# Perceiver layer on one core: GpSimd zero-writes between the 32 scatters of token rows to the experts

## The reference, cut to what matters

```python
logits = flat @ router_w.T
topk_scores, topk_idx = jax.lax.top_k(logits + router_bias, TOPK)      # TOPK = 2
topk_scores = jax.nn.softmax(topk_scores, axis=-1)
...
up_all = jnp.einsum('nd,kde->nke', flat, up_proj)
gate_all = jnp.einsum('nd,kde->nke', flat, gate_proj)
hidden = jax.nn.silu(gate_all) * up_all
down_all = jnp.einsum('nke,ked->nkd', hidden, down_proj)
out = jnp.einsum('nk,nkd->nd', combine, down_all)
sh_hidden = jax.nn.silu(flat @ sh_gate.T) * (flat @ sh_up.T)
out = out + sh_hidden @ sh_down.T
```

## Time and profile before

| what | value |
|---|---|
| three runs | 553.18, 553.84 and 561.45 us, median 553.84 us |
| profiled execution, its own time | 555.59 us |
| its span, from first to last instruction | 553.9 us |
| share of the span: PE, PEld, DVE, ACT, POOL | 89%, 61%, 71%, 34%, 36% |
| scatters, from the first start to the last end | 395.75 to 436.98 us |
| first tile loaded, first matmul of the experts | 438.63 and 440.83 us |

### The profile page before, as it was taken

The page is one execution under the profiler, slowest core; times in us unless marked ns, Lnnn a source line. Parts: engine busy times, 40 slices in busy tenths (PEclk is TensorE's granted clock), DMA queues, the critical chain, the costliest instruction groups (busy, mean ns, idle before and its releaser), DMA issues.

```text
span 553.9 us, 14401 instructions
## 1 busy us (share of the span) xinstructions
PE 493.0 (89%) x4952; PEld 335.8 (61%) x4953; DVE 394.4 (71%) x1038; ACT 190.6 (34%) x589; POOL 199.0 (36%) x302
## 2 busy tenths in 40 slices
PE   7897999999999999999997999999999299999900
PEld 7664666656656666666654666665466178888700
DVE  3798799999899999999544888887653135555525
ACT  3244332343323332333313455553200045555400
POOL 4000314011222222222115677773377435555520
PEclk9999999999999999999999999999999689999955
DMA  7999679877978888873128996700023334444258
GB/s 279 353 340 263 205 229 310 274 220 216 303 240 286 287 287 288 294 256 107 40 70 241 261 266 190 222 1 2 33 100 106 106 112 137 126 140 139 61 185 269
DMA packets 67296, 108.65 MB, mean 196 GB/s; under 512 B 8195, under 2 KB 49077, under 8 KB 67256
## 3 DMA queue, kind: packets, MB, share of 16 engines
q1 hardware_dynamic: 60840, 97.70, 56.7%
q0 software_dynamic: 3792, 8.43, 4.4%
q10 hardware_dynamic: 2624, 1.97, 1.1%
HBM read 85.31 MB, written 24.72 MB: 199 GB/s over the span
## 4 chain that ended last, share of the span: by engine, by line
PE 65%; DMA 10%; DVE 7%; POOL 7%; issue 6%; ACT 3%; SPq 1%; ACTq 0%; POOLq 0%; DVEq 0%
PE banks L1065 15%; PE banks L1041 14%; PE banks L1424 8%; DMA ring<-in_ctx_dram 7%; POOL rows_by_expert L711 6%; PE banks L1436 4%; DVE ctxT L1529 3%; PE banks L1053 3%; PE banks L1418 2%; PE banks L1000 2%; PE banks L1078 2%; DMA xn_all<-expert_out 2%; PE banks L1174 2%; PE banks L1181 2%; PE banks L1086 2%
## 5 line engine op out<-in xcount | busy, mean ns | idle before, releaser
L1529 DVE STREAM_TRANSPOSE ctxT<-ring 128x832 f32<-128x832 f32 x128 | 121.8, 1009 | 5.5 <-DMA ring<-in_ctx_dram 5.5
L1041 PE MATMUL banks<-ctxT,qT_all 32*64 32x416 f32 (+2 forms) x2048 | 93.9, 498 | 2.0 <-issue 1.2
L1065 PE MATMUL banks<-ring,prob 128*64 128x256 f32 (+1 forms) x832 | 93.6, 381 | 0.7 <-ACT prob L795 0.7
L1065 PEld LDWEIGHTS banks<-ring,prob 128*64 128x64 f32 (+1 forms) x832 | 58.6, 137 | 31.5 <-issue 4.2
L1041 PEld LDWEIGHTS banks<-ctxT,qT_all 32*64 32x64 f32 x2048 | 56.8, 131 | 30.7 <-issue 13.6
L611 POOL TENSOR_TENSOR var<-mv,eps 128x1 f32<-128x1 f32 x32 | 6.3, 196 | 168.9 <-DVE mv L1574 116.8
L717 POOL DMA_INDIRECT expert_out<-prob,dest x47 | 46.2, 984 | 46.4 <-DVE prob L1892 28.2
L808 ACT ACTIVATE prob<-banks,negmax 128x416 f32<-128x416 f32 (+2 forms) x80 | 41.0, 530 | 30.2 <-DVE negmax L1551 30.2
L1424 PE MATMUL banks<-ring,ctxT 128*128 x188 | 50.5, 392 | 0.3 <-ACT ctxT L919 0.3
L1885 DVE TENSOR_TENSOR ctxT<-banks,ctxT 128x128 f32<-128x128 f32 x47 | 13.7, 292 | 42.0 <-ACT ctxT L922 41.2
L795 ACT COPY prob<-banks 128x512 f32<-128x512 f32 x64 | 27.6, 515 | 38.9 <-PE banks L1053 38.9
(11 more groups left out here) (245 smaller groups left out, 876.6 us busy)
## 6 DMA issues: line engine op xcount, KB each, us to landing
ring<-in_ctx_dram SPq DMA_DIRECT2D x48, 1024.0 KB
qT_all<-q_by_pair SPq DMA_DIRECT2D x56, 128.0 KB, 8.9
ctxT<-rows_by_expert SPq DMA_DIRECT2D x47, 129.0 KB, 2.1
rows_by_expert<-blank SPq DMA_DIRECT2D x12, 387.0 KB, 4.4
mid<-stage SPq DMA_DIRECT2D x31, 128.0 KB, 2.3
ring<-in_ctx_dram SPq DMA_DIRECT2D x16, 130.0 KB
ctxT<-mid SPq DMA_DIRECT2D x16, 128.0 KB, 2.8
qT_all<-mid SPq DMA_DIRECT2D x16, 128.0 KB, 3.1
```

Of the source, the lines that this page charges most:

```text
L1041: last = pe.matmul(S[a][64 * b:64 * b + 64, 0:KW[a]], q_rep[mine, r, c, 64 * b:64 * b + 64], ctxT[mine, c, b, 0:KW[a]], start=c == 0, stop ...
L1065: last = pe.matmul(U[64 * b:64 * b + 64, 0:D], probT[0:rows, k, 64 * b:64 * b + 64], ring[0:rows, r, b, k, :], start=k == 0, stop=k == KT)
L1529: dve.transpose(ctxT[:, c].rearrange("p b (k j) -> p (b k) j", j=Q), ring[:, r].rearrange("p b k c -> p (b k) c")[:, :, columns(c):columns ...
```

## The change

Behind each of the 32 indirect transfers POOL writes zeros to a new buffer `pause` of 128 partitions by 256 float32. No instruction reads the buffer. Each write counts one on `zeroed`, and each write but the first waits until the write before it is counted, since both write the same bytes.

```diff
         head_max = sb("head_max", [P, HEADS])
+        pause = sb("pause", [P, D])
         head_sum = sb("head_sum", [P, HEADS])
...
                     c = g * TOPK + k
                     pool.indirect_dma_start(rows_dram, bass.IndirectOffsetOnAxis(ap=place_i[:, c:c + 1], axis=0),
                                             n2[k][:, g, :], None).then_inc(scattered, 16)
+                    if c:
+                        pool.wait_ge(zeroed, 5 + c)
+                    pool.memset(pause[:, :], 0.0).then_inc(zeroed, 1)
```

## The result

Over 20 runs of each kernel the changed one is slower by a factor of 1.0109 (95% interval 1.0082 to 1.0136): median 562.2 us against 558.1, where three runs of the kernel before had given 553.84. The interval makes that 4.6 to 7.6 us. The ratio leaves out executions that are more than 1.5% above the fastest of their kernel, and so do the medians given in the sections on the experiments; the two medians of all 20 runs lie 4.1 us apart. The profiled execution has a span of 564.3 us, 10.4 more than the one before; that is more than the interval allows, and what follows tells the two parts of it apart.

What follows compares the result with a forecast made beforehand. The prediction took POOL's chain of scatters, which every engine awaits from about 431 us, as the bound; 31 x 0.303 = 9.4 us on the 553.84 us median gave 563.2 us, with a range from 553.5 to 571.

Steps and rivals of the forecast that it cites:

- What bounds the kernel: From about 431 us every engine waits for POOL's scatters; each microsecond the last starts later ends the kernel one later.
- The write: Between scatters on POOL, 31 writes cost their full record of 0.303 us, 9.4 us in all; chance 0.60.
- the reading of the tenth scatter: On POOL, a record 0.75 us longer was followed by the usual 0.30 us gap, so longer work is added in full.
- the write hides in the gap: Rival: writes fit into the 0.30 us between scatters, cost 0.9 us, time 554.7 us; chance 0.20 with two other rivals.
- The waits: Between scatters on POOL, waits for the previous write cost nothing, at most 0.6 us for 31.
- Preparation exposed: Rival: scatter preparation can't run ahead across a write; 0.74 us each, 23 us, time 577 us; chance 0.20.
- The tail: Behind the last scatter, the last write costs nothing; PE's clock has already fallen, and later stages keep their length.
- the idle cover: POOL idles 12.80 us behind the last scatter until L717, hiding the last write; without it, 0.3 us once.
- the clock: PE's clock, already at its lower level by 434 us, returns some 6 us after work resumes; longer idling costs nothing more.
- The rival of a gain: Spacing avoids POOL's collisions with DVE at the tenth and first scatters, giving back 1.05 us, 552.8 us; within the shared 0.20.
- The landing place: Expected in the changed profile: scatter starts 1.57 us apart, last scatter at about 445.4 us, write record 0.303, idle 0.30.

Runs made afterwards that it cites:

- e1: Against the changed kernel, writes cut to 128x1, waits kept; step 1.265 us, ratio to the kernel before 1.0121, on chip A.
- e4: Against the changed kernel, no writes, each scatter waits for a count long reached; step 1.265 us, first scatter to end 166.4 us, chip A.
- e6: The kernel before, unchanged, traced on chip B; step 1.265 us, median of the kernel before there 564.9 us, this execution 570.1 us.
- e11: Against the kernel before, 32 extra scatters of two numbers a row ahead of the real ones, chip C; whole time 593.3 us.
- e5: The changed kernel once more, on chip B; ratio to the kernel before 0.9929, 561.0 us against 564.9.
- e9: Against the changed kernel, writes behind the first 22 scatters only, chip C; ratio to the kernel before 1.0033.
- e10: The changed kernel once more, on chip C; ratio to the kernel before 1.0063.
- e12: The kernel before, unchanged, traced on chip C; step 1.265 us, median 558.4 us.
- e7: Against the changed kernel, writes cut to 128x128, chip B; step 1.352 us, first scatter to end 164.9 us.

## Why the prediction was right or wrong

**The number.** Forecast were 563.2 us, measured 562.2, and that this is so close is luck. Two errors cancel: the three runs of the kernel before, at 553.84 us, were 4.3 below the 558.1 of all 20, and the 9.4 us put on top were too many, since the medians differ by 4.1 us, the ratio makes it 4.6 to 7.6, and the steps account for 6.0. As a change the forecast was 1.7% and the measurement 1.1%.

**What bounds the kernel.** Right where DVE is in time: the scatters' chain sets the end, and what they lose is lost in full (5.7 us more from first to last scatter, 5.8 from the first to PE's start). I took it for a property of the kernel, and it holds in some executions only: in the four traces with steps of 1.265 us on chips A and B the shared expert ends last, and covers the scatters' last microseconds.

**The write.** The mechanism was right in its direction, and the size was off. I put in 31 x 0.303 = 9.4 us, on the ground that the 0.30 us between scatters stay. Measured are 0.325 us for the write, but only 0.17 behind it, so 0.19 each and 6.0 in all. The step that failed is the reading of the tenth scatter: that no gap was eaten behind a longer *scatter* says that preparation waits for the scatter before it, and nothing about what can run beside that preparation. e1 shows that a write of 0.11 us can run beside it wholly, and the steps of the longer ones that 0.13 us of each do. The rival "the write hides in the gap" was half right: it hides as long as it is short, and the point where it stops hiding lies near 0.13 us of record and not at 0.30, because 0.17 us of the preparation do wait for the write's end.

**The waits.** Right: e4 shows no cost.

**Preparation exposed.** Not seen: the idle time in front of a scatter falls to 0.17 us and doesn't rise.

**The tail.** The last write and the idle cover were right (L721 starts 13.9 us after the last scatter, L717 13.8). So was the clock: it had fallen in both before PE resumed, and it came back 6.3 us after that instead of 6.1. The stages behind were to stay as long as before, and are 0.6 us longer in the first pair of traces, for a reason not found, and equal on chip C.

**The rival of a gain.** The one I gave, 1.05 us from collisions, gave back 0.3 us at the long scatter and nothing at the first: that record is 1.26 us in every trace whatever the spacing, so no run shows it to be a collision. The real gain is another: on chip B the spacing goes with counts of PE that are in time, worth 15 us between the last scatter and the experts in one pair of traces, and the change is faster by 0.7% there. I had argued that spaced scatters can't land sooner, and didn't ask what dense ones do to other engines. The trace of before could not have shown it, since it has no late start.

**The landing place.** Expected 1.57 us between starts, 445.4 for the last scatter; measured 1.457, and 445.70 only because the first started 4.0 us later, for a reason ahead of the scatters: luck again. The write's record was 0.325 us and not 0.303, and the idle time in front of a scatter 0.17 us and not 0.30.

## What to carry to other kernels

An instruction placed between two others on one engine costs its duration less what can run beside the idle time that stands there already. Time it at three lengths: the length at which the step begins to grow shows what is free. If engines next to a dense sequence of indirect transfers start late although what they need is long done, look at when the counts arrive; a short pause between transfers may pay for itself even on the critical path. Whether it is enough to put it only where the others still work wasn't tested. And time a change of this kind on more than one chip, because the same two kernels stood at 0.993 on one and at 1.006 on another.

## What the runs showed of the hardware

- A scatter starts 0.30 us after the end of the scatter before it or 0.17 us after the end of a write between the two, whichever is later. This held for writes of 0.11, 0.22, 0.325, 0.69 and 0.97 us. That these are two parts of one preparation is a reading, not shown.
- An indirect transfer of 128 rows holds POOL for 0.96 us, whether its rows have 8 or 1032 bytes.
- The first trace of the kernel before and those on one of three later chips have DVE in time beside scatters 1.265 us apart. On the other two it waits up to 17 us at a time in all four traces with this spacing, less in the one at 1.352 us and not at all in the three at 1.457 us or more. It waits for the counts of PE, which arrive up to 22 us after the matmuls' ends in e6. What holds them up stays open: e11 fell on a chip without the effect. A missing piece of program isn't it, since e6's queues of instructions moved nothing between 410 and 440 us. That it goes by the chip rather than by the moment isn't shown; only that on A and B the kernel before had medians of 568 and 565 us, and on C 558.
- The Trainium skill's page "SBUF — State Buffer" (Who interferes with whom) has a rule that fits another observation: a DVE instruction with two inputs in on-chip memory blocks a GpSimd instruction that reads it, and not one that only writes it. The long scatter record stands beside DVE's L1863 (L1867 after), which has two such inputs, in both traces: 407.38 to 408.32 under the scatter of 407.44, and here the changed kernel's

```profile
411.37 0.94 DVE L1867 TENSOR_TENSOR ring<-tile_no,tiles_to 1x768 f32<-1x768 f32 x1
```

  under the one of 411.71, which took 1.45 us. By that rule it would be the reading of the row numbers that waits, and the traces agree, with one thing more. In seven of the fourteen traces (before, after, e4, e5, e9, e10, e12) a scatter starts while this instruction of DVE has 0.58 to 0.89 us left, and each is longer than usual by what is left less 0.11 to 0.13 us. In the others none is long. There either no scatter starts beside it, or only one with 0.09 us left (e7), or one runs already, in e6 by as little as 0.04 us:

```profile
408.04 0.96 POOL L711 DMA_INDIRECT rows_by_expert<-xn_all,place_i  x1 [0.30 <-issue]
408.08 0.94 DVE L1863 TENSOR_TENSOR ring<-tile_no,tiles_to 1x768 f32<-1x768 f32 x1
```

  So a few hundredths of a microsecond decide over 0.5 to 0.8 us. That it is the reading isn't tested by itself.
